# Cross-attention in units of three key tiles: six score banks, and value products summed in SBUF

## What is computed

```python
qh = _layernorm((q @ Wq.T).reshape(B, Lq, H, D).transpose(0, 2, 1, 3), gq, bq) * D ** (-0.5)
kh = _layernorm((k @ Wk.T).reshape(B, Lk, H, D).transpose(0, 2, 1, 3), gk, bk)
vh = (v @ Wv.T).reshape(B, Lk, H, D).transpose(0, 2, 1, 3)      # k = v = context, H = 16, D = 32
attn = jax.nn.sigmoid(jnp.einsum('bhqd,bhkd->bhqk', qh, kh))
x = jnp.einsum('bhqk,bhkd->bhqd', attn, vh)
return x.transpose(0, 2, 1, 3).reshape(B, Lq, C) @ Wp.T + bp    # C = 512
```

## Time and profile before

| | |
|---|---|
| median of 3 runs | 2875.92 us (2872.34 to 2878.15) |
| profiled execution | 2869.23 us, its span 2867.5 us |
| TensorE busy | 2803.3 us, 98% of the span |
| VectorE, ScalarE, GpSimd busy | 1454.2, 1466.0, 885.6 us |
| mean granted clock of TensorE | 0.992 |

### The profile page before, as it was taken

How to read it: one execution, slowest core, us unless ns; L and a number is a source line. 1 busy time by engine, 2 the same in 40 slices (tenths; PEclk the granted TensorE clock), 3 DMA queues, 4 the chain that set the end, 5 groups by cost and what they waited for, 6 DMA issues and landing times.

```text
span 2867.5 us, 68578 instructions
## 1 busy us (share of the span) xinstructions
PE 2803.3 (98%) x27736; PEld 2263.2 (79%) x27736; DVE 1454.2 (51%) x2156; ACT 1466.0 (51%) x1465; POOL 885.6 (31%) x617
## 2 busy tenths in 40 slices
PE   4999999999999999999999999988999999999999
PEld 3777777777777777777777777757999998999998
DVE  5444444444444444444444444447577765567754
ACT  0455555555555555555555555535446565546554
POOL 2444444444444444444444444420000000000000
PEclk8999999999999999999999999999999999999999
DMA  5333333323333323333333333313545555555553
GB/s 209 87 82 85 85 81 86 88 80 85 84 82 86 87 80 85 85 82 86 86 81 85 85 82 86 84 45 111 190 162 191 191 193 193 196 185 189 179 200 127
DMA packets 194481, 334.48 MB, mean 117 GB/s; under 512 B 21736, under 2 KB 122344, under 8 KB 173040
## 3 DMA queue, kind: packets, MB, share of 16 engines
q1 hardware_dynamic: 194416, 333.56, 37.8%
HBM read 281.57 MB, written 51.90 MB: 116 GB/s over the span
## 4 chain that ended last, share of the span: by engine, by line
PE 92%; DVE 4%; issue 2%; DMA 1%; POOL 1%; ACT 1%; SPq 0%; POOLq 0%; DVEq 0%; ACTq 0%
PE kv_ps L1174 37%; PE f_ps L1455 23%; PE s_ps L1199 12%; PE o_ps L1211 12%; PE y_ps L1439 5%; PE mid_ps L1287 1%; DVE w_lo L729 1%; DMA k_dram<-k_blocks 1%; POOL k_var L479 1%; DVE pre L1041 0%; DMA k_rows<-k_dram 0%; ACT w_hi L583 0%; DMA wk_rows<-wk_dram 0%; DVE k_n L798 0%; PE kv_ps L1166 0%
## 5 line engine op out<-in xcount | busy, mean ns | idle before, releaser
L543 ACT ACTIVATE even_probs<-s_ps 128x2048 f32<-128x2048 f32 x196 | 368.9, 1882 | 513.8 <-PE o_ps L1211 348.8
L479 POOL TENSOR_TENSOR k_var<-k_var,neg_half 128x16 f32<-128x16 f32 x196 | 572.4, 2920 | 15.3
L543 ACT ACTIVATE odd_probs<-s_ps 128x2048 f32<-128x2048 f32 x196 | 370.1, 1888 | 193.8 <-PE s_ps L1199 193.8
L729 DVE TENSOR_TENSOR w_lo<-w_raw,w_hi 128x2048 fp32r<-128x2048 f32 x160 | 367.8, 2299 | 175.0 <-ACT w_hi L583 174.8
L469 POOL TENSOR_TENSOR ctx_lo<-ctx_raw,ctx_hi 128x512 fp32r<-128x512 f32 x196 | 253.1, 1291 | 621.9 <-DVE ctx_hi L772 621.9
L1455 PE MATMUL f_ps<-h_hi,w_hi 128*128 128x256 f32 x1536 | 427.5, 278 | 0.0
L1455 PE MATMUL f_ps<-h_lo,w_hi 128*128 128x256 f32 x1536 | 426.6, 278 | 0.0
L1455 PE MATMUL f_ps<-h_hi,w_lo 128*128 128x256 f32 x1536 | 426.5, 278 | 0.0
L791 DVE TENSOR_REDUCE k_var<-k_sq 128x16 f32<-128x496 f32 x196 | 131.4, 670 | 485.9 <-ACT k_sq L549 485.9
L583 ACT ACTIVATE w_hi<-w_raw 128x2048 fp32r<-128x2048 f32 x160 | 306.1, 1914 | 71.8 <-PE y_ps L1439 61.7
L1174 PE MATMUL kv_ps<-wk_hi,ctx_hi 128*128 128x496 f32 x784 | 324.7, 414 | 4.2 <-DVE q_lo L861 2.8
(11 more groups left out here) (215 smaller groups left out, 5009.1 us busy)
## 6 DMA issues: line engine op xcount, KB each, us to landing
w_raw<-w_dram SPq DMA_DIRECT2D x160, 1024.0 KB, 4.8
ctx_raw<-ctx_dram SPq DMA_DIRECT2D x196, 256.0 KB, 2.7
k_dram<-k_blocks SPq DMA_DIRECT2D x784, 64.0 KB, 1.8
k_rows<-k_dram SPq DMA_DIRECT2D x196, 256.0 KB, 3.0
qkv_w<-qkv_w_dram SPq DMA_DIRECT2D x1, 3072.0 KB, 13.6
bias_rows<-bias_rows_dram SPq DMA_DIRECT2D x1, 1280.0 KB, 16.8
wq<-wq_dram SPq DMA_DIRECT2D x1, 1024.0 KB, 5.7
wk_rows<-wk_dram SPq DMA_DIRECT2D x1, 1024.0 KB, 7.7
```

The costliest lines, as they stand in the source:

```text
L479: g.tensor_tensor(k_var[:, 2], k_var[:, 1], neg_half[:].to_broadcast([P, H]), ALU.pow)\
L543: s.activation(probs[r % 2][half][:], s_ps[:], ACT.Sigmoid).then_inc(probs_made, 1)
L729: v.tensor_tensor(w_lo[i][:], w_raw[i % RAW][:], w_hi[i][:].bitcast(f32), ALU.subtract)\
```

## The change

- **PSUM.** The score tile grows from four banks to six. `o_ps` gives its two banks up: it becomes another view of `kv_ps`, the projection's two banks.
- **Units.** Work goes in units `u` of three tiles (3u-2, 3u-1, 3u). Their twelve score groups make four runs of three groups; a run fills the six banks, and one sigmoid takes 128x3072. Groups of different row quarters must not write one bank at once, so a run's third group waits until the first has ended in the banks that it shares (`s_begun`).
- **Value products** of a unit are made at once (`attend_unit`), starting from zero, and VectorE adds the result to `o_sum` in SBUF (`sum_outputs`, two additions). Before the next projection TensorE waits for both (`free_of_outputs`).
- **Order.** TensorE: run 0, value products of the unit before, run 1, wait for the sums, projection(3u+1), run 2, projection(3u+2), run 3, projection(3u+3). VectorE's and ScalarE's as in the diff. GpSimd's and SyncE's steps keep their order, in loops of six tiles.
- **Buffers.** Three `kt` pairs in place of two, six `v_sb` in place of four, three `ctx_raw` in place of four; some borrow the room of `w_raw1`, whose first load moves behind the cross-attention. The matmuls that zeroed `o_ps` go.

```diff
+            def step(it, r, more=True):
+                put_keys(it, r)
+                if more:
+                    load_ctx(it, r + 3)
+                get_keys(it, r)
...
+            def sigmoid(it, u, run):
+                act.wait_ge(s_made, runs_of(it, u, run + 1))
+                if run == 0:
+                    wait(act, attended_first, unit_of(it, u))
+                else:
+                    wait(act, attended_high, unit_of(it, u))
+                s.activation(probs[run][:], s_ps[:], ACT.Sigmoid).then_inc(probs_made, 1)
...
+            def unit(it, u):
+                sigmoid(it, u, 0)
+                sigmoid(it, u, 1)
+                square(it, UNIT * u + 1)
+                sigmoid(it, u, 2)
+                square(it, UNIT * u + 2)
+                sigmoid(it, u, 3)
+                square(it, UNIT * u + 3)
...
             def copy_values(it, r):
-                dve.wait_ge(v_made, n_of(it, r, 1, 1))
-                wait(dve, av_made, n_of(it, r, 2, -4))
-                v.tensor_copy(v_sb[r % 4][:], kv_ps[:, 1]).then_inc(v_copied, 1)
+                dve.wait_ge(v_made, tile_of(it, r, 1))
+                if not isinstance(it, int) or r >= 2 * UNIT:
+                    dve.wait_ge(attended_high, unit_of(it, (r - 1) // UNIT, 0))
+                v.tensor_copy(v_sb[r % 6][:], kv_ps[:, 1]).then_inc(v_copied, 1)
...
-            def two_tiles(it, r):
+            def sum_outputs(it, u, first=False):
+                for half, attended, summed in ((0, attended_low, summed_low), (1, attended_high, summed_high)):
+                    part = slice(2 * half, 2 * half + 2)
+                    dve.wait_ge(attended, unit_of(it, u, 1))
+                    if first:
+                        v.tensor_copy(o_sum[:, part], o_ps[:, part]).then_inc(summed, 1)
+                    else:
+                        dve.wait_ge(summed, unit_of(it, u))
+                        v.tensor_tensor(o_sum[:, part], o_sum[:, part], o_ps[:, part], ALU.add).then_inc(summed, 1)
+
+            def step(it, r, split=True):
                 high_part(it, r + 1)
                 sum_squares(it, r)
-                split_keys(it, r - 1)
+                copy_values(it, r)
+                if split:
+                    split_keys(it, r - 1)
                 normalise(it, r)
-                copy_values(it, r)
-                high_part(it, r + 2)
-                sum_squares(it, r + 1)
-                split_keys(it, r)
-                normalise(it, r + 1)
-                copy_values(it, r + 1)
+
+            def unit(it, u, first=False):
+                sum_outputs(it, u - 1, first)
+                split_keys(it, UNIT * u)
+                step(it, UNIT * u + 1, split=False)
+                step(it, UNIT * u + 2)
+                step(it, UNIT * u + 3)
...
+            def slot(k, h):
+                if h < 2:
+                    return (h, k) if k < 2 else (4 + h, 1)
+                return (2 + h, 0) if k == 0 else (h, k - 1)
+
+            def scores(it, u, run):
+                wait(pe, probs_made, runs_of(it, u, run))
+                for k in range(UNIT):
+                    number = UNIT * run + k
+                    r, grp = UNIT * u - 2 + number // NG, number % NG
+                    if k == 0 or grp == 0:
+                        pe.wait_ge(kt_lo_made, tile_of(it, r, 1))
+                    ins = score_group(r, grp, k, runs_of(it, u, run + 1))
+                ins.then_inc(s_made, 1)
...
+            def score_group(r, grp, k, runs):
+                if k == 2:
+                    pe.wait_ge(s_begun, runs * 2)
+                hi, lo = kt_hi[r % 3], kt_lo[r % 3]
+                for n, (key, q) in enumerate(((hi, q_hi), (hi, q_lo), (lo, q_hi))):
                     for h in range(HG):
...
+                        if k == 0 and n == 2 and h >= 2:
+                            ins.then_inc(s_begun, 1)
+                return ins
...
+            def attend_unit(it, u):
+                first = UNIT * u - 2
+                pe.wait_ge(probs_made, runs_of(it, u, 4))
+                pe.wait_ge(v_copied, tile_of(it, first, 2 * UNIT))
+                pe.wait_ge(k_kept, tile_of(it, first, 2 * UNIT))
+                for grp in range(3):
+                    ins = attend(first, grp, grp, start=(grp != 1))
+                ins.then_inc(attended_first, 1)
+                for j in (1, 2):
+                    for grp in (0, 1):
+                        ins = attend(first + j, grp, NG * j + grp)
+                ins.then_inc(attended_low, 1)
+                attend(first, 3, 3)
+                for j in (1, 2):
+                    for grp in (2, 3):
+                        ins = attend(first + j, grp, NG * j + grp)
+                ins.then_inc(attended_high, 1)
+
+            def free_of_outputs(it, u):
+                pe.wait_ge(summed_low, unit_of(it, u, 1))
+                pe.wait_ge(summed_high, unit_of(it, u, 1))
+
+            def unit(it, u):
+                scores(it, u, 0)
+                attend_unit(it, u - 1)
+                scores(it, u, 1)
+                free_of_outputs(it, u - 1)
+                projection(it, UNIT * u + 1)
+                scores(it, u, 2)
+                projection(it, UNIT * u + 2)
+                scores(it, u, 3)
+                projection(it, UNIT * u + 3)
```

More of the change, by code:

```diff
@@ L159, in perceiver_block @@
             w_lo.append(sb(f"w_lo{i}", [P, CHUNK], f32r))
-        w_raw = [sb(f"w_raw{i}", [P, CHUNK]) for i in range(RAW)]
+        w_raw = [sb("w_raw0", [P, CHUNK])]
+        lent = ExitStack()
+        kt_hi, kt_lo = [sb("kt_hi2", [P, NG, P], f32r, lent)], [sb("kt_lo2", [P, NG, P], f32r, lent)]
+        v_sb = [sb(f"v_sb{i}", [P, C], f32, lent) for i in (4, 5)]
+        lent.close()
+        w_raw.append(sb("w_raw1", [P, CHUNK]))
+        o_sum = sb("o_sum", [P, NG, TOK])
         x = sb("x_rows", [P, TT, C])
@@ new lines, in _ @@
+            for r in range(UNIT):
+                square(0, r)
+            act.wait_ge(s_made, 1)
+            s.activation(probs[0][:], s_ps[:], ACT.Sigmoid).then_inc(probs_made, 1)
+            square(0, UNIT)
+            act.wait_ge(s_made, 2)
+            s.activation(probs[1][:, 0:4], s_ps[:, 0:4], ACT.Sigmoid).then_inc(probs_made, 1)
+            with act.Fori(0, (last_unit - 1) // 2) as it:
+                unit(it, 1)
+                unit(it, 2)
+            for run in range(4):
+                sigmoid(0, last_unit, run)
@@ L774, in split_keys @@
+                wait(dve, v_made, tile_of(it, r, -1))
+                v.tensor_copy(ctx_hi[r % 2][:], raw[r % 3][:]).then_inc(ctx_hi_made, 1)
             def split_keys(it, r):
                 dve.wait_ge(k_moved[r % 2], moved(it, r))
-                wait(dve, s_made, n_of(it, r, 2, -2))
-                hi, lo = (k[r % 2][:].rearrange("p g (b k) -> p b g k", b=HG) for k in (kt_hi, kt_lo))
+                if not isinstance(it, int) or r >= UNIT:
+                    u, place = (r - 1) // UNIT, (r - 1) % UNIT
+                    dve.wait_ge(s_made, runs_of(it, u, place + 2))
@@ L864, in _ @@
             copy_values(0, 0)
-            high_part(0, 2)
-            sum_squares(0, 1)
-            split_keys(0, 0)
-            normalise(0, 1)
-            copy_values(0, 1)
-            two_tiles(0, 2)
-            with dve.Fori(0, nq - 1) as it:
-                two_tiles(it, 4)
-                two_tiles(it, 6)
-            two_tiles(nq - 1, 4)
-            two_tiles(nq - 1, 6)
-            split_keys(nq, 3)
-            dve.wait_ge(av_made, 2 * (NKT + 1) - 1)
-            v.tensor_copy(o_t[:, 0:2], o_ps[:, 0:2]).then_inc(once("o_low"), 1)
+            for r in range(1, UNIT + 1):
+                step(0, r)
+            unit(0, 1, first=True)
+            unit(0, 2)
+            with dve.Fori(0, (last_unit - 5) // 2) as it:
+                unit(it, 3)
+                unit(it, 4)
+            unit(0, last_unit - 2)
+            unit(0, last_unit - 1)
+            sum_outputs(0, last_unit - 1)
+            split_keys(0, NKT - 1)
+            sum_outputs(0, last_unit)
             dve.wait_ge(once("x_offset"), 1)
@@ L1260, in _ @@
-            scores(nq, 3, 1)
-            for half in range(2):
-                attend(nq, 3, half)
+            projection(0, 1)
+            projection(0, 2)
+            pe.wait_ge(kt_lo_made, 1)
+            for grp in range(3):
+                ins = score_group(0, grp, grp, 1)
+            ins.then_inc(s_made, 1)
+            projection(0, 3)
+            pe.wait_ge(probs_made, 1)
+            pe.sem_inc(s_begun, 2)
+            score_group(0, 3, 1, 2).then_inc(s_made, 1)
+            scores(0, 1, 0)
@@ new lines, in _ @@
+            projection(0, 6)
+            unit(0, 2)
+            with pe.Fori(0, (last_unit - 3) // 2) as it:
+                unit(it, 3)
+                unit(it, 4)
+            first = UNIT * last_unit - 2
+            scores(0, last_unit, 0)
+            attend_unit(0, last_unit - 1)
+            scores(0, last_unit, 1)
```

(11 more changed lines are left out.)

255 lines of the change are left out of this document (102 added, 153 removed).

## The result

The changed kernel takes 3060.97 us in the median of 4 runs (3059.96 to 3064.2), the kernel before 2874.61 us (4 runs). The ratio is 1.0649, 95% interval 1.0631 to 1.0667: slower, as forecast, and 10 us under the forecast of 3071. The profiled execution took 3059.96 us, its span 3058.2.

The account below looks back on a forecast made before the run. The keys' loop was to replace TensorE as bound: 26.2 us for early tiles, 63 units x 31.22 and 31.2 at the end made 2024.3, +197.2; with sigmoids 3067.7, plus half of 6.7, 3071 us; range 3015 to 3145.

Parts of the forecast that it names:

- The loop of the keys: Cross-attention: normalising, transposing, DRAM round trip and split of keys set the period, 31.22 us a unit against TensorE's 27.35.
- the GpSimd leg: From the split to k_n of tile 3u+1, low_part and deviation run in series behind the split: 6.07 us, formerly 1.07.
- the round trip: From k_n to the split of the same tile, with transpose, four puts, a get and both landings: 7.67 us.
- the three slower cases: The main forecast, the clock rival and the third rival: slower by over 0.2%, given 92% together.
- TensorE's gain: TensorE's cross-attention work: fewer switches between matmul shapes, 27.35 us a unit against 28.05, 0.70 saved.
- s_begun at nothing: TensorE's wait before a score run's third group: covered by group 1, taken as 0, allowed 0 to 0.8 us a unit.
- The sums at nothing: Two o_sum additions awaited before the next projection, 0.69 us each: taken as 0, uncovered 1.4 us a unit.
- Where TensorE would stand: TensorE's idle time: about 1.5 us inside run 1, 1.7 before a unit's first projection, 1 or so before the second.
- Another sign: VectorE at k_centred/k_n of every third tile: waits on GpSimd's k_var for about 5 us.
- TensorE stays the bound: Rival in cross-attention: keys' loop under 28.05 us a unit; 45 us less, 2824, or 2875 with s_begun's cost; chance 6%.
- The clock rival: TensorE's clock falls in new standstills, giving 32.8 us of work a unit; 100 us more, 3170; chance 9%.
- The third rival: The keys' loop binds but is shorter, 29.5 us a unit; 93 us more, 2962; chance 4%.

Follow-up runs that it names:

- run 1: Not a follow-up kernel: the second of a unit's four score runs on TensorE, after the value products of the unit before; up to 1.48 us in the best kernel.
- run 2: Not a follow-up kernel: the third of a unit's four score runs on TensorE, after projection(3u+1); 1.54 to 1.70 us in every second unit of the best kernel.
- the order alone: The kernel before, with VectorE's split_keys(r-1) moved ahead of high_part(r+1) and sum_squares(r) in every second tile: 3229.56 us, ratio 1.1228.
- the best kernel: The changed kernel with high_part and sum_squares back ahead of the split, and separate TensorE waits for the sums' low and high halves: 2839.14 us, ratio 0.99.
- the kernel with the old order: The changed kernel with VectorE's high_part and sum_squares moved back ahead of the split at each unit's first tile: 2885.02 us, ratio 1.0028.
- the waits taken apart: The changed kernel with TensorE awaiting the low sum before the projection's K part, the high sum only before its V part: 3065.54 us, ratio 1.0681.

## Why the prediction was right

**The loop of the keys.** Shown by three experiments in both directions: the order alone makes the old kernel slow, undoing it takes 176 of 186 us back, and a longer trip costs three times its growth a unit. The period was 30.95 us in the unit shown and 30.99 on average, 31.22 predicted; the GpSimd leg 6.10 against 6.07. The term that was off is the round trip, 7.58 on average where I took 7.67. From the first split (69.25) to the last (2081.87) there were 2012.6 us where I had summed 2024.3.

**The 10 us between forecast and median** come from errors that partly cancel, which is luck. The stage took 12 us less than summed. From the last split to the end the profiled execution had 976.3 us where the kernel before had 971.5: 4.8 more, where I had added 1.3, and 0.4 more lay ahead of the first split; no run takes these apart. The median lay 1.0 above the profiled execution; I had given half of 6.7 for that, a guess. Two slips in the rivals bore on nothing: the three slower cases have 94% together and not 92, and the 2824 and 2962 start from the profiled 2869 while the forecast of 3071 starts 3 us above it.

**TensorE's gain.** Right in kind and too large: 0.5 in place of 0.70 a unit, once both loops were out of the way. The trace of that kernel shows where most of the last 0.2 went. TensorE's timeline, then VectorE's:

```profile
1011.91 0.28 PE L1255 MATMUL s_ps<-q_hi,kt_lo 32*128 32x256 f32 x4
1012.22 0.39 PE L1255 MATMUL s_ps<-q_hi,kt_hi 32*128 32x256 f32 x4
```

```profile
1011.39 0.69 DVE L801 TENSOR_TENSOR kt_lo<-k_rows,kt_hi 128x512 fp32r<-128x512 f32 x1
```

The third group of run 2 starts 0.31 us behind the row before, where 0.12 is usual, and 0.14 behind the end of its kt_lo. From 900 to 1280 us this comes in every second unit: run 2 takes 1.54 to 1.70 us to the next projection and not 1.28. In some of the same units run 1 takes up to 1.48, with the low sum under way meanwhile. Together this is 0.2 us a unit. So a little of both waits is left, though TensorE hardly ever counts as idle for it.

**s_begun at nothing.** In the best kernel TensorE is busy 99.8% of the stage with this wait in place, and in the profile after the groups around it start at 1000.97, 1001.08, 1001.23 and 1001.35. One step is 0.15 in place of 0.117, so the wait costs at most some 0.03 us a run there; no kernel ran without the wait. The sigmoid over 3072 columns took 2.74, not 2.8, and was hidden.

**The sums at nothing.** True for the changed kernel, where they lie in VectorE's wait for the keys. Not true in general: in the kernel with the old order they are what makes the second loop 28.23. I had priced them as cover for a score run and not as a leg of a loop.

**Where TensorE would stand** was half wrong. I expected 1.5 us inside run 1, 1.7 before the first projection, 1 before the second. The wait before the first came in every unit, 1.7 to 1.9 us. A wait for kt_lo is nowhere in TensorE's table of waits from 300 to 2000 us. The rest depends on the clock. In the unit shown the first projection ran partly at the lower clock: 1031.08 - 1023.94 = 7.14 us to the next run, 1.5 more than 5.64, so TensorE arrived later everywhere and had less to wait for. Of the 55 units from 300 to 2000 us 27 are like this one; in the other 28 the first projection takes 5.6 and TensorE stands later on, as in the next unit: 0.59 us before the second projection (1062.84, on ctx_lo) and 0.84 before the value products (1077.56, on v_sb), which I had not listed. In all it idles 2.7 us a unit and not 4, and is busy 91%, not under 90%. Another sign was too large: the idle time of VectorE before k_n of every third tile is 3.0 us on average (88 us in 29 units), not 5, since VectorE has work of its own in the rest of the leg.

**The rivals.** That TensorE stays the bound fell with the trace. The clock rival's mechanism happened in half of the units, for 3 us in the one shown and not a whole projection. The profile has stretches of either kind to compare, each from one unit's first projection to that of five units later:

```profile
621.51:776.38 154.87, 138.36 (x1561) 105.93 (x1561) 65.44 (x115) 71.73 (x51) 65.33 (x45) 1.00 0.29 76
1179.50:1334.25 154.75, 145.19 (x1560) 111.14 (x1561) 65.89 (x115) 71.21 (x51) 65.49 (x45) 0.94 0.28 76
```

At 1.00 five units take 154.87 us, at 0.94 they take 154.75. TensorE is busy 7 us longer in the second, and all of it went into its room of 3.9 us a unit, as the argument against this rival said. The third rival, a shorter loop, was right in sign only: 30.99 us a unit, not 29.5. Why the trips are 0.09 shorter than in the kernel before was not tested.

## What to carry to other kernels

A tuned kernel whose main engine is 100% busy can have another loop right behind it, here 8.74 us a tile under 9.35. List the loops that go round through several engines and a transfer, with the order of each engine's queue as one of the links, and sum each one before an instruction is moved ahead of or behind a wait. A wait in an in-order queue belongs behind everything that other engines are waiting for. And a fix that shows nothing may be standing behind another loop: the waits taken apart gained nothing alone and some 37 us once the order was right.

## What the runs showed of the hardware

TensorE's clock did not go by the length of one standstill. In the earlier trace rows, behind 3.81 us without work, it was 0.50 from 1897 to 1899 us. In the changed kernel TensorE stood 1.7 to 1.9 us once in every unit, behind the same value products and score run each time; in 27 of 55 units the projection behind it took 7.0 to 7.2 us, in 28 it took 5.6. In the unit shown the granted clock was 0.50 (the 1.2 GHz level) from 1024 to 1027 us:

```profile
1024.00:1027.00 3.00, 3.00 (x8) 2.42 (x9) 0.00 (x0) 0.92 (x1) 0.00 (x0) 0.50 0.58 152
1027.00:1031.00 4.00, 4.00 (x18) 3.12 (x16) 2.04 (x4) 1.06 (x2) 0.83 (x1) 0.96 0.17 55
```

In the kernel with the waits apart alone, where no wait of TensorE's was longer than 1.2 us from 300 to 1900 us, it was 1.00 in all that time. What makes the difference between the two kinds of unit, no run here shows.

The cost of one more transfer in a chain was more than its step in the queue. In the changed kernel a fifth put of 64 KB, like the four behind it, was issued 0.38 us ahead of them and lengthened the trip by 0.54 us on average, from 7.58 to 8.12; in the kernel before it was 0.43, from 7.67 to 8.10.
